# Fp32 rows through router and gather, the fp16 halves made behind the experts' transposes

## The reference

```
x = x + tanh(g_xattn) * attention(layernorm(x), ctx, ctx)     # 32 query heads, 8 key heads, D = 32
h = layernorm(x)
scores = softmax(h @ w_cls.T)                                  # 64 choices: 32 experts, 32 that do nothing
top 8 of scores + bias; w = 1.5 * scores / sum                 # a gate per token and choice
routed = sum over the experts chosen of w * (silu(h @ Wg) * (h @ Wu)) @ Wd   # H 1024, I 512, up to 512 tokens
x = x + tanh(g_ffn) * routed * (1 + sum of w over the choices that do nothing)
```

## Time and profile before

| | |
|---|---|
| median of three runs | 2426.59 us |
| the profiled execution | 2429.58 us |
| its span, first to last instruction | 2427.9 us |
| PE busy | 2126.0 us, 88% |
| DVE busy | 1511.0 us, 62% |
| ACT busy | 1303.4 us, 54% |
| POOL busy | 866.1 us, 36% |
| mean granted clock of PE | 0.957 |

### The profile page before, as it was taken

The page is one execution under the profiler, slowest core; times in us unless marked ns, Lnnn a source line. Parts: engine busy times, 40 slices in busy tenths (PEclk is TensorE's granted clock), DMA queues, the critical chain, the costliest instruction groups (busy, mean ns, idle before and its releaser), DMA issues. The chain is left out here.

```text
span 2427.9 us, 45912 instructions
## 1 busy us (share of the span) xinstructions
PE 2126.0 (88%) x15296; PEld 1266.4 (52%) x15297; DVE 1511.0 (62%) x2730; ACT 1303.4 (54%) x1894; POOL 866.1 (36%) x893
## 2 busy tenths in 40 slices
PE   4988888888889942999999989899989899989976
PEld 2554555555555531445656665554655676554454
DVE  4779988988898762334644665553464775553373
ACT  3787777777777640333544554452453664443364
POOL 3013454554445555013423442331241443221152
PEclk9999999999999966999999999999999999989998
DMA  4354433444343253366776878585594898767563
GB/s 116 91 162 116 129 111 105 125 129 130 117 122 90 93 157 105 105 156 168 205 205 160 197 201 219 129 249 139 141 273 125 225 250 213 202 148 204 142 156 91
DMA packets 456170, 376.43 MB, mean 155 GB/s; under 512 B 109654, under 2 KB 377046, under 8 KB 456080
## 3 DMA queue, kind: packets, MB, share of 16 engines
q1 hardware_dynamic: 411024, 303.27, 43.7%
q0 software_dynamic: 45056, 72.09, 14.0%
HBM read 310.94 MB, written 101.06 MB: 170 GB/s over the span
## 5 line engine op out<-in xcount | busy, mean ns | idle before, releaser
L1388 PE MATMUL psum<-xgt,wgu 128*128 128x256 f16 (+3 forms) x6144 | 858.9, 303 | 31.8 <-DVE wgu L1057 21.8
L1388 PEld LDWEIGHTS psum<-xgt,wgu 128*128 128x128 f16 x6144 | 550.3, 99 | 339.1 <-DVE wgu L1057 23.8
L556 POOL TENSOR_TENSOR spare<-spare 128x1 f32<-128x1 f32 x264 | 132.9, 504 | 1088.5 <-PE psum L1397 457.3
L1397 PE MATMUL psum<-wdn,apair 128*128 128x512 f16 x1944 | 458.2, 387 | 49.7 <-ACT ys L839 40.6
L922 DVE TENSOR_REDUCE mx<-psum 128x2 f32<-128x512 f32 x512 | 329.7, 687 | 101.0 <-PE psum L1232 90.2
L1133 DVE COPY xgt<-psum 128x1024 f16<-128x1024 f16 x256 | 168.1, 688 | 300.4 <-PE psum L1373 278.3
L839 ACT ACTIVATE ys<-psum,slots 128x512 f32<-128x512 f32 x256 | 162.9, 690 | 317.4 <-PE psum L1397 314.6
L1143 DVE SCALAR_TENSOR_TENSOR a<-psum,sg 128x512 f32<-128x512 f32 x128 | 88.2, 689 | 388.2 <-PE psum L1388 388.2
L1397 PEld LDWEIGHTS psum<-wdn,apair 128*128 128x128 f16 x1944 | 186.8, 99 | 252.2 <-issue 43.0
L750 ACT ACTIVATE prob<-psum 128x512 f32<-128x512 f32 x512 | 276.4, 595 | 70.5 <-PE psum L1245 61.2
L1057 DVE SCALAR_TENSOR_TENSOR wgu<-wraw,wgu 128x1024 f16<-128x1024 f32 x256 | 311.7, 1219 | 0.5 <-ACT wgu L767 0.5
(11 more groups left out here) (131 smaller groups left out, 1992.2 us busy)
## 6 DMA issues: line engine op xcount, KB each, us to landing
wraw<-in_L_ffn_w_gate_up_dram SPq DMA_DIRECT2D x256, 512.0 KB, 5.6
wraw<-in_L_ffn_w_down_dram SPq DMA_DIRECT2D x128, 512.0 KB, 6.6
x<-in_x_dram SPq DMA_DIRECT2D x16, 1024.0 KB
qs<-qh SPq DMA_DIRECT2D x256, 64.0 KB
xr<-in_x_dram SPq DMA_DIRECT2D x16, 1024.0 KB
out_dram<-x SPq DMA_DIRECT2D x16, 1024.0 KB
pairs<-xs SPq DMA_DIRECT2D x16, 1024.0 KB, 4.1
qs<-ql SPq DMA_DIRECT2D x128, 64.0 KB
```

Source lines behind the costliest of these rows:

```text
L1388: mm = pe.matmul(ps_gu[:, s, h, 0:nt * P], w[:, a, k, :], xgt[:, c, k, 0:nt * P], start=(k == 0 and (a, c) == (0, 0)), stop=(k == KB - 1 a ...
L1397: mm = pe.matmul(psum[:, Y_BANK[i] + n2, :], apair[:, o, k, c * P:(c + 1) * P], w[:, a, k, :], start=(k == 0 and (a, o) == (0, 0)), stop=( ...
```

## The change

The normed rows stay fp32 in the router, in DRAM and in the gather. `hi_x` writes only xn; `low_x` is gone; `store_rows` stores xn, 4 KB per token as before. X transposes are four fp32 ones per unit (half the columns of 128 tokens), the logits 16 fp32 products of 64 columns, lg is copied out of PSUM. In the expert stage PE transposes fp32 rows, four transposes per unit; ACT's new `take_hi` rounds a unit into xgt's hi half; `take_t` (DVE) subtracts that from the bank and writes the lo half. take_hi stands on ACT ahead of `y_out` of block i = 3. On the ScalarE side also: its loop in the attention stage gets the hint, `take_heads` comes ahead of `q_stack` 3 in slot 7, and `norm_q` ahead of `m_rows` and `x_stack` in slots 1 and 2. X1 moves on PE from behind K0 to the end of slot 0.

```diff
-            sp.wait_ge(xs_ready, 2 * b + 2)
-            sp.dma_start(pairs_v[b], xs[:].rearrange("p t a h -> p t (a h)")).then_inc(pairs_out, 16)
+            sp.wait_ge(xhi_ready, 2 * b + 2)
+            sp.dma_start(rows_v[b], xn[:]).then_inc(rows_out, 16)
...
-                for to in (xs[:, t, 0, :], xn[:, t]):
-                    act.activation(to, x2[:, t], ACT.Identity, scale=rstd[:, 1, t:t + 1],
-                                   bias=nmr[:, 1, t:t + 1]).then_inc(xhi_ready, 1)
+                act.activation(xn[:, t], x2[:, t], ACT.Identity, scale=rstd[:, 1, t:t + 1],
+                               bias=nmr[:, 1, t:t + 1]).then_inc(xhi_ready, 1)
...
-                act.activation(xt[:, u % 2, u // 2].rearrange("p k s -> p (k s)"), ps_x16[x],
+                act.activation(xt[:, u // 2, 4 * (u % 2):4 * (u % 2) + 4].rearrange("p k s -> p (k s)"), ps_x[x],
...
-                    if kv == 7 and on(b, 2):
-                        q_stack(b + 2, 3)
                     if kv < 2 and on(b, -1):
                         take_heads(b - 1, kv + KV - 2)
                     if kv >= 2 and on(b, 0):
                         take_heads(b, kv - 2)
+                    if kv == 7 and on(b, 2):
+                        q_stack(b + 2, 3)
+                    if kv in (1, 2) and on(b, 2):
+                        norm_q(b + 2, kv - 1)
                     if kv == 1 and on(b, 0):
                         m_rows(b, 1)
                     if kv < 3 and on(b, -2):
                         x_stack(b - 2, kv + 1)
-                    if kv in (1, 2) and on(b, 2):
-                        norm_q(b + 2, kv - 1)
...
-            loops(act, step)
+            loops(act, step, mybir.EngineType.Activation)
...
+            def take_hi(e, u):
+
+                c, k = u // 2, 4 * (u % 2)
+                act.wait_ge(gt_full, 8 * e + u + 1)
+                act.wait_ge(gt_free, 8 * e + u - 1 + FREE)
+                act.activation(xgt[:, 0, k:k + 4, c * P:(c + 1) * P], ps_g[u % 2].rearrange("p (k t) -> p k t", k=4),
+                               ACT.Copy).then_inc(gh_ready, 1)
...
                 for i in range(CT):
                     for n2 in range(2):
+                        if i == CT - 1 and not last:
+                            for u in range(4 * n2, 4 * n2 + 4):
+                                take_hi(e + 1, u)
                         y_out(e, par, i, n2)
...
-            def low_x(b, t):
-                dve.wait_ge(xhi_ready, 4 * b + 2 * t + 2)
-                dve.tensor_tensor(xs[:, t, 1], xn[:, t], xs[:, t, 0], ALU.subtract).then_inc(xs_ready, 1)
...
-                dve.tensor_reduce(lg[:], ps_x[x][:, 0:2 * T2 * NALL].rearrange("p (t a e) -> p t e a", t=T2, a=2),
-                                  AXX, ALU.add).then_inc(x_free[x], 1)
+                dve.tensor_copy(lg[:].rearrange("p t e -> p (t e)"), ps_x[x][:, 0:T2 * NALL]).then_inc(x_free[x], 1)
...
-                c, part = u // 2, u % 2
-                dve.wait_ge(gt_full, 8 * e + u + 1)
-                dve.tensor_copy(xgt[:, part, :, c * P:(c + 1) * P],
-                                ps_g16[u % 2].rearrange("p (k t) -> p k t", k=KB)).then_inc(gt_free, 1)
+                c, k = u // 2, 4 * (u % 2)
+                dve.wait_ge(gh_ready, 8 * e + u + 1)
+                dve.tensor_tensor(xgt[:, 1, k:k + 4, c * P:(c + 1) * P], ps_g[u % 2].rearrange("p (k t) -> p k t", k=4),
+                                  xgt[:, 0, k:k + 4, c * P:(c + 1) * P], ALU.subtract).then_inc(gt_free, 1)
...
-                for k in range(KB):
-                    mm = pe.transpose(px[:, k * P:(k + 1) * P], xs[:, u // 2, u % 2, k * P:(k + 1) * P], ident[:])
+                for k in range(4):
+                    at_k = 4 * (u % 2) + k
+                    mm = pe.transpose(px[:, k * P:(k + 1) * P], xn[:, u // 2, at_k * P:(at_k + 1) * P], identf[:])
...
-                    for part in range(2):
-                        for k in range(KB):
-                            mm = pe.matmul(px[:, t * 2 * NALL:(t + 1) * 2 * NALL], xt[:, part, t, k, :],
-                                           wc[:, k].rearrange("p a e -> p (a e)"), start=(part == 0 and k == 0),
-                                           stop=(part == 1 and k == KB - 1))
+                    for k in range(KB):
+                        mm = pe.matmul(px[:, t * NALL:(t + 1) * NALL], xt[:, t, k, :], wc[:, k],
+                                       start=(k == 0), stop=(k == KB - 1))
...
-                    if kv == 0 and on(b, -2):
-                        x_transpose(b - 2, 1)
                     valued(kv, 0)
...
-                    if kv in (1, 2) and on(b, -2):
+                    if kv in (0, 1, 2) and on(b, -2):
                         x_transpose(b - 2, kv + 1)
...
-                for k in range(KB):
-                    mm = pe.transpose(ps_g16[u % 2][:, k * P:(k + 1) * P], xg[:, c, part, k * P:(k + 1) * P], ident[:])
+                for k in range(4):
+                    at_k = 4 * (u % 2) + k
+                    mm = pe.transpose(ps_g[u % 2][:, k * P:(k + 1) * P], xg[:, c, at_k * P:(at_k + 1) * P], identf[:])
```

More of the change, by code:

```diff
@@ L644, in gather @@
                     pool.indirect_dma_start(
-                        out=xg[:, c].rearrange("p a h -> p (a h)"), out_offset=None, in_=pairs,
+                        out=xg[:, c], out_offset=None, in_=rows,
                         in_offset=bass.IndirectOffsetOnAxis(ap=gslots[:, par, c, 0:1].bitcast(U32), axis=0),
@@ L676, in _ @@
             act.activation(tgate[:], gates[:], ACT.Tanh).then_inc(setup_act, 1)
-            act.activation(wcpair[:, 0, :], wcraw, ACT.Copy, scale=W_SCALE).then_inc(setup_act, 1)
             act.wait_ge(consts, 2)
@@ L856, in step2 @@
                     for n2 in range(2):
+                        if i == CT - 1 and not last:
+                            for u in range(4 * n2, 4 * n2 + 4):
+                                take_hi(e + 1, u)
                         y_out(e, par, i, n2)
+            for u in range(8):
+                take_hi(0, u)
             loops2(act, step2)
@@ L869, in link @@
                 tally.wait()
-            dve.wait_ge(setup_act, 2)
+            dve.wait_ge(setup_act, 1)
             dve.tensor_copy(tg_at[:], tgate[:, 0:1]).then_inc(setup_dve, 1)
             dve.tensor_scalar(tg_ff[:], tgate[:, 1:2], ROUTE_SCALE / (A_SCALE * W_SCALE), None, ALU.mult).then_inc(setup_dve, 1)
[L874 to L877, removed]
-                dve.tensor_copy(wc[:, :, u, :], ps_x16[0][:, 0:KB * NALL].rearrange("p (k e) -> p k e", k=KB)).then_inc(setup_dve, 1)
+            dve.wait_ge(wc_t, 1)
+            dve.tensor_copy(wc[:].rearrange("p k e -> p (k e)"), ps_x[0][:, 0:KB * NALL]).then_inc(setup_dve, 1)
             dve.wait_ge(consts, 2)
-            dve.wait_ge(setup_dve, 5)
+            dve.wait_ge(setup_dve, 3)
             def carry_wait(tally):
@@ L1086, in step @@
                         norm_shift(1, nth_norm2(b - 1))
-                    if kv == 6 and on(b, -1):
-                        low_x(b - 1, 0)
                     scored(kv, 1)
@@ L1107, in step @@
                         router_b(b - 2, tally)
-                    if kv == 6 and on(b, -1):
-                        low_x(b - 1, 1)
                     if kv == 6 and on(b, -2):
@@ L1176, in _ @@
             pe.wait_ge(consts, 2)
-            pe.wait_ge(setup_act, 2)
+            pe.wait_ge(small_in, 64)
+            for k in range(KB):
+                mm = pe.transpose(ps_x[0][:, k * NALL:(k + 1) * NALL], wcraw[:, k * P:(k + 1) * P], identf[0:NALL, 0:NALL])
+            mm.then_inc(wc_t, 1)
             pe.wait_ge(setup_dve, 3)
-            for u in range(2):
-                if u:
-                    pe.wait_ge(setup_dve, 4)
-                for k in range(KB):
-                    mm = pe.transpose(ps_x16[0][:, k * NALL:(k + 1) * NALL], wcpair[:, u, k * P:(k + 1) * P], ident[0:NALL, 0:NALL])
-                mm.then_inc(wc_t, 1)
-            pe.wait_ge(setup_dve, 5)
             def take_bank(name, b):
```

44 lines of the change are left out of this document (22 added, 22 removed).

## The result

The changed kernel takes 2489.85 us (median of four runs, 2487.93 to 2493.47), the one before 2426.68 beside it: the ratio is 1.0261 [1.0244, 1.0279], 63 us slower. The forecast was 2473, 46 slower, in a range of 2440 to 2512. The span of its profiled execution is 2491.8 us.

What follows compares the result with a forecast made beforehand. PE was taken to bound the kernel, clearly in the expert stage, with DVE nearly as busy in attention. Attention -37 us and expert stage +83 sum to +46, giving 2473 us, range 2440 to 2512.

Steps and rivals of the forecast that it cites:

- The mechanism of the expert stage: Expert boundaries: PE's third unit waits for DVE, DVE for ACT's take_hi behind six y_out; +61 us.
- The chain at an expert's start: Experts of four or three blocks: a 0.6 us eviction enters the chain before first products; 14 x 0.6, +8 us.
- PE's clock: Expert stage: new stalls bring slower products after them, at 4/7 x 1.2 us for nine stalls, plus 2; together +8 us.
- fp32 transposes: Expert stage: four fp32 transposes per unit replace eight; 114 units x 0.04, +5 us on PE.
- The first expert: Expert stage: the very first expert's eight units pass through two engines; +1 us.
- The attention stage: Whole first stage: -20 for the hint, -16 for 13 full steps, -1 after the last batch; -37 us.
- 16 were forecast for all of them: Attention stage, 13 full steps: half of less waiting minus added PE work, 1.2 us less per step; -16 us.
- (a) The hint on ACT's loop: Attention stage, ACT's four jumps back: long steps become as short as the others, 4 x (55.4 - 50.3); -20 us.
- Up to 4.5 us of PE's waiting in a step: Attention stage: later X1 and less ACT and DVE work remove up to 4.5 us of PE's waits per step.
- the 120 to 125 taken: Attention stage, fp32 logits: 32 records bound by loads of 120 to 125 ns, 4.0 us; +2.0 us per step.
- The 107 ns: Router logits: the skill page's estimate for a plain 128-column load at 1.2 GHz; logits 3.4 us, total 8 us lower.
- rival 2: Attention stage: DVE's in-order queue sets the step, so +2.8 us a step, 52 more, 2525; chance 0.08.

Runs made afterwards that it cites:

- Experiment 1: The changed kernel with ACT's take_hi moved ahead among the six ys evictions instead of behind all six; 2433.65 us, ratio 1.0029.
- experiment 3: The changed kernel without the hint on ACT's loop; 2490.38 us, ratio 1.0262.
- experiment 5: The kernel before with the hint on ACT's loop alone; 2416.49 us, ratio 0.9955.
- experiment 7: The kernel before with X1 moved to the end of slot 0 on PE alone; 2405.31 us, ratio 0.9911.
- 4: The kernel before, fp16 halves kept, with the hint, take_heads and norm_q moved ahead, and X1 late; 2401.05 us, ratio 0.9895.
- 6: The kernel before with take_heads ahead of q_stack 3 in slot 7 alone, no hint; 2422.30 us, ratio 0.9976.
- 9: The kernel before, fp16 halves kept, with X1 late, take_heads and norm_q moved ahead, no hint, on another chip; 2454.60 us, ratio 0.9945.
- 11: The changed kernel with DVE's two 1.2 us subtractions per step put back into an unread tile, on another chip; 2570.23 us, ratio 1.0418.
- 12: Second run of the changed kernel with DVE's two 1.2 us subtractions per step put back into an unread tile; 2567.73 us, ratio 1.0390.
- 10: The kernel before with X1 late and the hint on ACT's loop, on another chip; 2456.78 us, ratio 0.9950.

## Why the prediction held, and where its steps failed

**The mechanism of the expert stage: right.** The burst, the three engines in a row and the sizes came out as worked out: 2.80 for 2.9 us behind two blocks, 1.63 for 1.8, 0.47 for 0.5, 2.57 for 2.8. With the counts 9, 6, 9 and 7 that is 25.2 + 9.8 + 4.2 + 18.0 = 57 us for the 61 of the forecast. Experiment 1 shows it by taking most of it away: the stage became 60.6 us shorter (1571.3 to 1510.7), 48 idle and 13 busy.

**The chain at an expert's start: right.** 1.75 for 1.12 us in eight experts and 0.46 for nothing in six are 7.8 us, for the 8 of "14 x 0.6"; the ninth expert with four blocks is the first, below.

**PE's clock: the term was mis-sized.** Forecast +8. These are the groups of PE in the expert stage, before, after, and in experiment 1:

```profile
L1397 PE MATMUL psum<-wdn,apair 128*128 128x512 f16 x1944 | 458.2, 387 | 49.7 <-ACT ys L839 40.6 <-issue 9.1
...
L1373 PE MATMUL psum<-ident,xg 128*128 128x128 f16 x1408 | 110.5, 230 | 50.9 <-DMA xg<-pairs,gslots 44.7 <-DVE wdn L1062 6.2
```

```profile
L1389 PE MATMUL psum<-wdn,apair 128*128 128x512 f16 x1944 | 468.4, 393 | 49.5 <-ACT ys L835 38.2 <-issue 11.3
...
L1365 PE MATMUL psum<-identf,xg 128*128 128x128 f32 x704 | 120.2, 309 | 110.5 <-DVE xgt L1130 59.4 <-DMA xg<-rows,gslots 45.1 <-DVE wdn L1063 6.0
```

```profile
L1390 PE MATMUL psum<-wdn,apair 128*128 128x512 f16 x1944 | 458.5, 387 | 49.8 <-ACT ys L835 38.2 <-issue 11.5
...
L1366 PE MATMUL psum<-identf,xg 128*128 128x128 f32 x704 | 113.3, 297 | 62.2 <-DMA xg<-rows,gslots 45.2 <-DVE xgt L1131 13.3 <-DVE wdn L1064 3.7
```

The down products took 10 us more and gave them back in experiment 1, the transposes 7 of their 10: 17 us that come and go with the stalls. The gate and up products took 3 us more than before and kept them (858.9, 862.2, and 864.8 in experiment 1), so that some 13 are left for the whole of PE, where the forecast had 8. The window of the stall above shows where:

```profile
1156.20:1168.00 11.80, 8.60 (x42) 4.85 (x39) 4.39 (x7) 7.09 (x13) 0.90 (x2) 0.86 1.10 333
```

It has a granted clock of 0.86. I took the lower level to follow 4 times in 7 from stalls of 3 us; it followed eight of the nine stalls of 2.80 to 2.85 us.

**fp32 transposes: +3 us for +5.** 113.3 for 110.5 in experiment 1, where the stalls are gone.

**The first expert: undersized.** Forecast +1. PE's timeline, its first products, before and after:

```profile
960.45 41.61 PE L1388 MATMUL psum<-xgt,wgu 128*128 128x512 f16 x192 [1.08 <-DVE xgt L1133]
```

```profile
932.01 44.18 PE L1380 MATMUL psum<-xgt,wgu 128*128 128x512 f16 x192 [1.70 <-DVE xgt L1130]
```

They start 11.5 us behind the first transposes for 9.2, with a last wait of 1.70 us where it was 1.08, and then take 2.6 more. In both kernels PE has stood 44 or 45 us before the first transposes, and the lower clock lasts on behind them: after it is 0.50 up to 937.2 us, 5.2 us into these products, before it had risen ahead of them (1.00 from 960.45 on). Together +4.9. A further 1.9 is an "issue" wait of PE at the second expert, 7.34 us for 5.43, which the forecast did not have.

**The attention stage: the total was near (-31 for -37), the steps behind it were not.** That the sum came out so near is luck. The four long steps gave 16 us (55.1 to 51.1 on average), though not by the hint; the other full steps gave some 2, where 16 were forecast for all of them; and some 12 came from the first and last steps, where the forecast had 1. "(a) The hint on ACT's loop ... -20 us" failed. Nothing of it is seen in the change's medians (experiment 3), and it is 12 us alone on the kernel before (experiment 5). The long steps are 51.1 us with the hint and without it. The mistake was to give the stop of 2.23 us in the earlier trace rows the whole difference between long and short steps. PE's 4.07 us at X1 had a second condition, that X1 stood right behind K0; moving it was worth 23 us of the stage with ACT's stop still there (experiment 7). The hint and the move clear the same wait, and their gains do not add (experiments 4 to 7).

"Up to 4.5 us of PE's waiting in a step", half of it kept, failed too. The step is 50.8 us on average (51.1 and 50.5), where the short one was 50.3: forecast 49. Between 4, with fp16 rows, and the changed kernel lie only 3.8 us of the first stage (924.37 to 920.53), and they come from its first and last steps: the full steps are 0.4 us longer than those of 4 (50.80 for 50.39). What left ACT and DVE, four activations and subtractions of 1.2 us, was paid back on PE by the logits. Their size was right: 3.79 us, a load of the path every 114 ns for the 120 to 125 taken. These are the loads between 200 and 800 us:

```profile
L1287 PEld LDWEIGHTS psum<-wc,xt 128*128 128x128 f32 x384 | 43.8, 192 | 4.6 <-issue 4.6
```

The 107 ns that I estimated from the Trainium skill (TensorE: Matmul & The Clock Gate, LDWEIGHTS (loading the stationary operand)) lie 7 below the measured 114, about as far off as my row's 120 is above; it would have given 3.4 us of logits for the measured 3.79.

What PE waits for changed with it. The waits, 200 to 800 us, after:

```profile
PE psum L1225 <- DVE mx L928: 37.8, 91, 1.5
...
PE psum L1238 <- ACT prob L746: 4.5, 12, 0.4
```

Before, PE stood 25.8 us for ACT's exponentials and 27.0 for xt. Both are gone or small, and 37.8 us for DVE's maxima, in 91 pieces, stand there where it was 8.0. Emptying one queue let PE run into the other; rival 2 was right in that much, and wrong in its +2.8 us a step.

**Still open.** Why the changed kernel has no stop at ACT's jump back and 18 packets less without the hint (experiment 3), where 6, 7 and 9 on the fp16 code have both. Its loop has fewer instructions on ACT (286 records in the trace of 3 for a trip, 290 before), but no run varied that by itself. And the worth of DVE's relief, as said at 11 and 12. The 1.9 us at the second expert have no cause shown either.

## What to carry to other kernels

When work moves to an engine that is half idle, look up where it stands in that engine's order: here ACT had the time, and with the rounding behind a burst the expert stage was 95 us longer than before, with most of the burst behind the rounding 34. The order was worth 60 us; of the 34 left, 22 are waits of the longer chain. When two edits clear the same wait, their gains do not add; take the wait, not the edit, as the unit of the sum, and test each edit by itself, since a bundle can hide that one part (the orders, -26 us) is good and another (the rounding behind the burst, +56) is not. A short new wait on PE can cost more than itself, through its clock: here 48 us of waits cost 13 us of busy time on top.

## What was not expected of the hardware

The same program on another chip was 1.8% slower: 2470.31 us for 2427 to 2429 on the two others. In nearly every step there ACT waits 1.4 to 1.8 us for its own instructions, which on the other chips it does at its jumps alone or not at all, but for once each in experiments 4 and 7. With the hint the stop at the jumps is 1.4 us there (10), without it 2.5 (9), and the others are left.

These waits are not the whole difference. Between 4 and 9 lie 53 us, 24 in the first stage and 29 in the expert stage. There PE too stands longer before its gate and up products, and is busy longer at them; 4, then 9:

```profile
L1386 PE MATMUL psum<-xgt,wgu 128*128 128x256 f16 (+3 forms) x6144 | 860.4, 303 | 31.8 <-DVE wgu L1057 21.6
```

```profile
L1386 PE MATMUL psum<-xgt,wgu 128*128 128x256 f16 (+3 forms) x6144 | 872.4, 305 | 45.6 <-DVE wgu L1057 21.4
```

The 13.8 us of idle time that 9 has more are waits for "issue", 13.6 us in 31 pieces that 4 does not have. No trace of the kernel before was taken on that chip, so that the same holds for its 1.8% is not shown. A price for a hint read on one chip is therefore not one for all, and kernels are compared only beside the kernel before on the same chip.
